# Moving the first-half score matmuls of odd attention steps ahead of the even step's projection

## What is computed

```python
xn = layernorm(x)                       # no scale, no shift
# attention, 128 heads, head size 4, latent 64, "rope" part 64
c_q, c_kv = xn @ Wq_down, xn @ Wkv_down
q_c = (c_q  @ Wq_up).reshape(b, s, 128, 4)
k_c = (c_kv @ Wk_up).reshape(b, s, 128, 4)
v_c = (c_kv @ Wv_up).reshape(b, s, 128, 4)
q_r = (xn @ Wq_rope).reshape(b, s, 128, 64)
k_r = xn @ Wk_rope                      # shared by all heads
scores = (q_c . k_c + q_r . k_r) / sqrt(68)
out = softmax(scores) @ v_c  -> reshape -> @ Wo
# result
y = x + out * silu(ffn(xn))             # ffn: silu(lin1) * lin3 -> lin2, each with rank-2 part
```

## Time and profile before

| what | value |
|---|---|
| median of 3 runs | 2130.03 us (2130.02 to 2134.33) |
| the profiled execution | 2131.2 us, span 2129.3 us |
| TensorE matmuls, weight loads | 2043.9 us (96%), 1551.4 us (73%) |
| VectorE | 1417.2 us (67%) |
| ScalarE | 1014.0 us (48%) |
| GpSimd | 465.7 us (22%) |
| DMA | mean 40 GB/s |

### The profile page before, as it was taken

One profiled execution on the slowest core, in us unless ns is written; L12 is line 12 of the kernel. 1 busy time (PEld: TensorE's weight loads), 2 busy tenths in 40 slices (PEclk: granted clock), 3 DMA queues, 4 the chain that ended last, 5 costly groups with the idle time before them and its releaser, 6 DMA issues. The chain is left out here.

```text
span 2129.3 us, 39329 instructions
## 1 busy us (share of the span) xinstructions
PE 2043.9 (96%) x12768; PEld 1551.4 (73%) x12768; DVE 1417.2 (67%) x1770; ACT 1014.0 (48%) x1446; POOL 465.7 (22%) x802
## 2 busy tenths in 40 slices
PE   6799999999999999999999999999999999977998
PEld 4577777777777777777777777777777777755776
DVE  5366676666766666766767766667667667636774
ACT  2345454555555554545554555455555455443222
POOL 1112121212222122212121212121212121123221
PEclk8899999999999999999999999999999999999999
DMA  4211111111111111112121111111111111131221
GB/s 136 76 17 38 29 32 33 31 31 28 36 27 37 20 42 22 41 23 42 20 42 22 41 23 34 27 33 31 32 33 30 32 27 28 24 107 62 89 84 44
DMA packets 117607, 85.50 MB, mean 40 GB/s; under 512 B 48646, under 2 KB 91654, under 8 KB 117566
## 3 DMA queue, kind: packets, MB, share of 16 engines
q1 hardware_dynamic: 117566, 84.97, 18.0%
HBM read 41.93 MB, written 16.78 MB: 28 GB/s over the span
## 5 line engine op out<-in xcount | busy, mean ns | idle before, releaser
L636 DVE TENSOR_REDUCE mx<-sx 128x4 f32<-128x1024 f32 x512 | 627.2, 1225 | 525.4 <-PE sx L727 521.3
L608 ACT ACTIVATE probs<-st 128x1024 f32<-128x1024 f32 x512 | 501.4, 1025 | 217.9 <-PE st L710 217.9
L590 ACT ACTIVATE slot<-pj 64x512 fp32r<-64x512 f32 x512 | 303.2, 592 | 591.9 <-PE pj L740 585.6
L526 POOL CAST k<-kc 64x512 fp32r<-64x512 f32 x256 | 183.9, 719 | 1300.0 <-PE st L710 1299.8
L740 PE MATMUL pj<-xh,wh 128*128 128x512 f32 x1024 | 408.6, 399 | 23.9 <-DVE slot L646 23.9
L710 PE MATMUL st<-slot,k 89*128 89x512 f32 x1024 | 423.8, 414 | 1.1 <-DMA slot<-mrow 1.1
L710 PE MATMUL st<-slot,krlh 128*128 128x512 f32 x1024 | 406.2, 397 | 0.0
L740 PE MATMUL pj<-xl,wh 128*128 128x512 f32 x1024 | 401.4, 392 | 0.0
L740 PE MATMUL pj<-xh,wl 128*128 128x512 f32 x1024 | 400.6, 391 | 0.0
L646 DVE TENSOR_TENSOR slot<-pj,slot 64x512 fp32r<-64x512 f32 x512 | 353.1, 690 | 20.1 <-ACT slot L590 4.0
L727 PEld LDWEIGHTS sx<-k,slot 88*128 88x128 f32 x2048 | 312.1, 190 | 60.9 <-issue 19.8
(11 more groups left out here) (161 smaller groups left out, 1408.8 us busy)
## 6 DMA issues: line engine op xcount, KB each, us to landing
w_stage<-in_Wq_rope SPq DMA_DIRECT2D x64, 256.0 KB, 3.1
o_scratch<-o_sb SPq DMA_DIRECT2D x128, 64.0 KB, 2.1
k<-kc SPq DMA_DIRECT2D x128, 48.0 KB
slot<-kc SPq DMA_DIRECT2D x256, 24.0 KB
k<-kx SPq DMA_DIRECT2D x128, 48.0 KB
slot<-kx SPq DMA_DIRECT2D x256, 24.0 KB
x_in<-in_x SPq DMA_DIRECT2D x4, 1024.0 KB, 7.2
v_scratch<-probs SPq DMA_DIRECT2D x4, 1024.0 KB, 4.3
```

Of the source, the lines that this page charges most:

```text
L526: nc.gpsimd.tensor_copy(k1[0:64, s, :, :].rearrange("p a n -> p (a n)"), krh[:, bp * CH:(bp + 1) * CH]).then_inc(k_ready, 1)
L590: nc.scalar.activation(slot1[0:64, (k - 1) % NS, e, :, :], pj[64 * e:64 * e + 64, :].rearrange("p (a n) -> p a n", a=2), ACT.Copy).then_in ...
L608: nc.scalar.activation(probs[:, s, kt], st[:, kt], ACT.Exp, scale=SCALE).then_inc(exp_done, 1)
L636: nc.vector.tensor_reduce(mx[:, p, lo:lo + 4], sx[:, :, :].rearrange("p a (b k) -> p (a b) k", b=2), axis=AX.X, op=ALU.max).then_inc(red_d ...
```

## The change

The function `scores` now takes the half kt as an argument and does one half. In an even body both halves of step k-4 stay where they were, and the first half of step k-3, which is an odd step, is added between the row scores and the projection. In an odd body only the second half of step k-4 is left. ScalarE's exponentials follow the same order: three in an even body, one in an odd one. Nothing is added or removed in number, no DMA is moved, and the code of VectorE, GpSimd and SyncE is the same.

```diff
@@ ScalarE, body @@
                 if at.live(k - 4) and k - 4 < STEPS:
-                    v = at.step(k) - 4
-                    if at.live(k - 8):
-                        act.wait_ge(av_done, v - 3)
-                    if at.first and k == 7:
-                        act.wait_ge(v_stored, 16 * NC)
-                    for kt in range(2):
-                        act.wait_ge(st_done, 2 * v + kt + 1)
-                        nc.scalar.activation(probs[:, s, kt], st[:, kt], ACT.Exp, scale=SCALE).then_inc(exp_done, 1)
+                    if k % 2 == 0:
+                        exponentials(at, k - 4, 0)
+                    exponentials(at, k - 4, 1)
+                if k % 2 == 0 and at.live(k - 3) and k - 3 < STEPS:
+                    exponentials(at, k - 3, 0)
...
+            def exponentials(at, k, kt):
+                v = at.step(k)
+                if kt == 0 and at.live(k - NS):
+                    act.wait_ge(av_done, v - 3)
+                if kt == 0 and at.first and k == NS - 1:
+                    act.wait_ge(v_stored, 16 * NC)
+                act.wait_ge(st_done, 2 * v + kt + 1)
+                nc.scalar.activation(probs[:, k % NS, kt], st[:, kt], ACT.Exp, scale=SCALE).then_inc(exp_done, 1)
@@ TensorE, scores: one half per call @@
-            def scores(at, k):
+            def scores(at, k, kt):
...
-                pe.wait_ge(mrow_in[s // 2], 16 * (at.turn(k) + 1))
-                pe.wait_ge(ql_done, 2 * v + 2)
-                pe.wait_ge(s2_done, v + 1)
-                for kt in range(2):
-                    if at.live(k - 1):
-                        pe.wait_ge(exp_done, 2 * v - 1 + kt)
...
+                if kt == 0:
+                    pe.wait_ge(mrow_in[s // 2], 16 * (at.turn(k) + 1))
+                    pe.wait_ge(ql_done, 2 * v + 2)
+                    pe.wait_ge(s2_done, v + 1)
+                if at.live(k - 1):
+                    pe.wait_ge(exp_done, 2 * v - 1 + kt)
...
@@ TensorE, body @@
                 if at.live(k - 4) and k - 4 < STEPS:
-                    scores(at, k - 4)
+                    if k % 2 == 0:
+                        scores(at, k - 4, 0)
+                    scores(at, k - 4, 1)
                 if at.live(k - 1) and k <= STEPS:
                     row_scores(at, k - 1, 0)
+                if k % 2 == 0 and at.live(k - 3) and k - 3 < STEPS:
+                    scores(at, k - 3, 0)
                 if k < STEPS:
                     project(at, k)
```

More of the change, by code:

```diff
@@ L695, in transpose_maxima @@
                 nc.tensor.transpose(sx[0:16, 0, 0:128], mx[:, (k // 2) % 2, :], ident[:, :]).then_inc(mt_done, 1)
-            def scores(at, k):
+            def scores(at, k, kt):
                 s, v = k % NS, at.step(k)
                 b = 2 * ((k // NS) % NBP)
-                pe.wait_ge(mrow_in[s // 2], 16 * (at.turn(k) + 1))
-                pe.wait_ge(ql_done, 2 * v + 2)
-                pe.wait_ge(s2_done, v + 1)
-                for kt in range(2):
-                    if at.live(k - 1):
-                        pe.wait_ge(exp_done, 2 * v - 1 + kt)
[L706 to L712, removed]
+                if kt == 0:
[4 more added lines that the diff above has]
+                    pe.wait_ge(exp_done, 2 * v - 1 + kt)
+                for h in range(2):
+                    ks = (b + h) * S + kt * 128
+                    for n, (kk, q, n_rows) in enumerate(((k1[0:KC + 1, s, h, kt * 128:kt * 128 + 128], slot1, KC + 1),
+                                                         (krlh[:, ks:ks + 128], slot2, 128))):
+                        last = nc.tensor.matmul(st[:, kt, h, :].rearrange("p (e n) -> p e n", e=PH), kk,
+                                                q[0:n_rows, s, :, h, :], start=(n == 0), stop=(n == 1))
+                last.then_inc(st_done, 1)
             def row_scores(at, k, half):
```

## The result

| | before | after |
|---|---|---|
| median (lowest to highest), 5 runs each | 2132.19 us (2130.02 to 2135.78) | 2142.0 us (2139.5 to 2143.41) |
| profiled execution, span | 2131.2 us, 2129.3 us | 2141.58 us, 2139.7 us |
| ratio after/before, 95% interval | | 1.0044 [1.0029, 1.0059] |

The change makes the kernel 0.4% slower, by 9.8 us between the medians and 10.4 us between the profiled executions. The forecast was 2130.1 with a range up to 2139: the time lies 3 us outside, on the slower side. About 2 of the 11.9 us by which the forecast missed come from its base, since the median of the kernel before is 2132.19 in five runs and was 2130.03 in the three that the prediction had; 9.8 lie between the medians.

The account below looks back on a forecast made before the run. TensorE's work was taken as the bound, so only its standstills could change: -43.3 us in even bodies, +43.0 in odd ones and +0.4 at the end sum to +0.1, giving 2130.1 us, range 2116 to 2139.

Parts of the forecast that it names:

- The wait is gone, with 0.38 to spare: Even bodies with k%4=0: the moved scores let VectorE's subtraction finish before the projection is due; 64 waits vanish.
- a new stall of 0.33 us: Odd bodies: row scores, with four score matmuls less ahead, wait for VectorE's copy of the maxima; +43.0 us over 126 bodies.
- 56 in the loop at 0.68: Loop's even bodies with k%4=0: each removed projection wait saves 0.68 us, 0.57 of waiting plus 0.11 of restart.
- Four take 1006.12 - 1005.17 = 0.95 us: Time of the four moved score matmuls, which would delay the even body's projection from 1007.52 to 1008.47.
- 8 in straight-line code at 0.73: First and last groups of 16 steps: eight removed projection waits save 0.73 us each, as release is slower there.
- 28 odd bodies at 0.38: Odd bodies whose wait for the maxima stands on its own instruction: 0.16 plus 0.22 us of slower release each.
- -0.6 and +0.1: Last group, up to the last projection: predicted change of -0.6 us against a measured +0.1.
- After the last projection ... +0.4: End of attention: the last step's four scores find the exponential still running and come 0.42 us late, +0.4.
- rival 3: Even bodies: the exponential, with slack 0.13 us, becomes the bound; at 0.20 late the kernel takes 2153; chance 0.08.
- rival 1: Odd bodies: the waiting row scores' weight load is done before VectorE's copy ends; net -13.8, 2116 us; chance 0.15.
- rival 2: Odd bodies: every row-score wait has the slow latency, 47.9 us instead of 43.0; 2135 us; chance 0.22.
- the gain of 43.3: Even bodies: total predicted saving in us from removing 64 projection waits, in the loop and in straight-line code.

Follow-up runs that it names:

- The earlier copy: Changed kernel with VectorE copying the transposed maxima between its two subtractions instead of after both: 2098.59 us, ratio 0.983 to the kernel before.
- the later copy: Changed kernel with VectorE's 0.69 us copy of slot1 put ahead of its copy of the maxima: 2238.17 us, ratio 1.0481 to the kernel before.
- VectorE's copy moved there: Kernel before, with VectorE's copy of the maxima moved between its two subtractions, as a control: 2133.6 us, ratio 0.9997.
- the wait for the maximum put last: Changed kernel with TensorE's operand waits placed ahead of the row scores' wait for the maximum: 2142.81 us, ratio 1.0035 to the kernel before.
- The two kernels with one half of the change each: Kernel before with scores moved only into bodies with k%4=0 (first): 2122.0 us, 0.9942; only into those with k%4=2 (second): 2157.98 us, 1.0113.
- the same with the early table load: Changed kernel with maxima copied between the subtractions, maximum's wait last, and a one-element Exp before the first content copy: 2095.37 us, ratio 0.982.

## Why the prediction was wrong

The mechanism in the loop was right and the forecast fell to its sizes: it was a difference of two terms of 43 us each, so that an error of 0.04 us in a term that occurs 56 or 126 times is 2 to 5 us of the result. Step by step:

- **"The wait is gone, with 0.38 to spare"**: right. 65 waits became one.
- **"a new stall of 0.33 us"**, 98 times in the loop: right. It is .319 and .335, with 98 waits named. Of its parts, 0.21 is the late start, 0.10 the restart and 0.01 to 0.02 a slower projection. The earlier copy takes the stall away and the later copy lengthens it, which shows that it hangs on this copy.
- **"56 in the loop at 0.68"**: mis-sized. The even body gains 0.636. The sum took the row scores at 0.48 once the wait was gone, since the view of before shows 0.48 in other bodies. They take 0.534, because the weight load of the first is held back: the sequencer has four instructions to do at the maximum's end, which the projection's wait had covered. That is a stall under a stall, the very thing the prediction looked for in odd bodies and not here. The earlier trace rows has it: the row scores at 1007.04 last 0.70 there, where undisturbed ones last 0.64. It is 0.044 x 56 = 2.5 us.
- **"Four take 1006.12 - 1005.17 = 0.95 us"**, taken as all that the move costs a body: mis-sized. The four themselves take 0.935, but with k%4=2 the projection behind them slows from 2.723 to 2.774, and the body is 0.051 longer: 2.9 us in 56 bodies. The prediction asked in these bodies only whether the exponential would be late. It was not.
- **"8 in straight-line code at 0.73"** and 28 odd bodies at 0.38: mis-sized. In straight-line code the even bodies with k%4=0 gain 0.67, since their moved four take 1.01 and not 0.95; with k%4=2 they lose 0.10; and the odd ones lose 0.40. That is +0.2 per four steps, where the sum had 0.03, and in the last group this makes up the 0.7 us between -0.6 and +0.1.
- **The first group, predicted with the same rates**: the term for the first exponential was missing. From the first score matmul on it is +2.0 and not +0.1. About 1.0 is the moved scores' wait for the exponential behind the table load, 0.3 the odd body behind it, and some 0.6 the rates above. Another execution of each order repeats it: from the first scores to the projection of k = 15 it is 80.26 us before and 80.23 with VectorE's copy moved there, 82.29 after the change and 82.30 with the wait for the maximum put last.
- **The start, ahead of the first scores**: no matmul is moved there, and the two traces differ all the same, by -1.2 us up to the first projection and +1.0 from there to the first scores. The projection of k = 3 runs at half pace after the change, with 0.43 between its matmuls, the lower of TensorE's two levels (1.2 GHz), and only in part so before. The stretch from 106 to 114 us, before and after (last but two is the granted clock):

```profile
106.00:114.00 8.00, 5.68 (x22) 4.74 (x23) 4.19 (x7) 0.70 (x2) 0.00 (x0) 0.79 0.10 15
```

```profile
106.00:114.00 8.00, 6.93 (x22) 5.79 (x23) 2.89 (x5) 0.62 (x2) 0.00 (x0) 0.57 0.09 15
```

  No moved matmul stands ahead of it. The two kernels with one half of the change each, which differ from one another only behind this point, show both pictures: the first has 0.57 there and 0.43 between all twelve matmuls, the second 0.79 and 0.43 between the first five. So it is a difference between executions.
- **"After the last projection ... +0.4"**: measured +1.5, and from another cause. The moved half of the last odd step makes its scores ask sooner for the row of maxima, and TensorE waits for the DMA 1.98 where it waited 1.05 before; in this execution the score matmuls after that go at 0.43:

```profile
1887.91 0.71 PE L716 MATMUL st<-slot,k 89*128 89x512 f32 x1 [1.98 <-DMA slot<-mrow]
1888.41 0.63 PE L716 MATMUL st<-slot,krlh 128*128 128x512 f32 x1
1888.84 0.63 PE L716 MATMUL st<-slot,k 89*128 89x512 f32 x1
```

  Not all of the 1.5 is the change's. From the last projection to the end of attention before takes 21.8 us, the change 23.3. Two kernels from above, the whole change with the maximum's wait last and the same with the early table load, have one order here and take 22.3 us, with a granted clock of 1.00 in the 9.5 us where these scores lie, and 23.5 us, with 0.82. Before has 1.00 there and the change 0.82. So with an undisturbed clock it is +0.5, and the other 1.0 is a difference between executions. The forecast of 0.4 was near the 0.5 by luck, since it had reckoned with another wait.
- **The exponential with its slack of 0.13** (rival 3): it never became the bound in the loop. Its one case is the one in the first group, above.
- **The cheap restart** (rival 1) is refuted: a weight load of the waiting row scores is not done ahead. It starts with its matmul, and R is .575 instead of .475 in the odd bodies where the wait stands on the matmul. The Trainium skill, TensorE: Matmul & The Clock Gate, section "Step-by-step: what each phase is for", says that weight loads are pulled ahead of matmuls in flight. The traces agree where nothing is waited for (before, this weight load starts at 1015.13 and its matmul at 1015.36), and not at the semaphore wait, where both start at 1006.67 and the restart costs 0.10 us.
- **The dear release** (rival 2) stood at 2135. The odd bodies did not have it, except the one with k = 1 in each turn (1.33 instead of 1.24) and those in straight-line code (1.33 too), as the prediction had counted them. The result lies beyond that rival all the same, for the other reasons.

The range was too narrow on the slow side: it held bounds for the new stall, but none for the gain of 43.3, nothing for the bodies with k%4=2, and nothing for the start, where a change of order meets a ScalarE that has yet to load its table. Nor had it room for a clock that differs by a microsecond or two between executions at the start and the end of attention.

## What to carry to other kernels

Work that fills a wait in one place uncovers a chain in the place it came from. Before moving it, look at which instruction ends that chain and whether its engine could do it sooner; here a copy of 0.28 us put ahead of an independent subtraction turned a loss of 10 us into a gain of 36. Move only what a wait can take: the half of this move that filled nothing cost 23.5 us. And when a forecast is a difference of two large terms, read each place where a stall is removed for the next stall under it (what started late, but was covered?), and give both terms bounds.

## What the runs showed of the hardware that was not expected

- TensorE's sequencer took about 0.1 us for each instruction between the end of what it waited for and the weight load: 0.40 us for four, the waiting one included (1011.91 to 1012.31), where a wait that stands on the matmul itself releases it in 0.05 (1006.62 to 1006.67). The order in which waits are written was worth time where the last to come stood first: with it put last, R is .473 instead of .534.
- The restart of weight load and matmul after a wait cost 0.10 us when the row scores were 0.21 late and no more when the later copy made them 0.93 late (R .575 and .58).
- The pace of a long projection depends on what came before it: from 2.723 to 2.774 for the same twelve matmuls at a granted clock of 1.00. No run here explains it; it is worth up to 2.9 us.
- At the start and at the end of attention, where TensorE stood still for 1.3 to 2.6 us at a time, the granted clock was at the lower level for stretches whose length differed between executions with the same order of matmuls. From 106 to 114 us it was 0.57 with the first half of the change and 0.79 with the second, with matmuls 0.43 apart instead of 0.23. Behind the last projection it was 1.00 in one of two executions and 0.82 in the other. Differences of 1 us between single traces of these stretches tell nothing of an edit.
